# Delta rule: decay and key products of the chunk ahead placed inside the refinement steps, and its key blocks' transfers ahead of the inverse's

## The reference, cut to what matters

```python
def step(S, inputs):
    q_t, k_t, v_t, g_t, b_t = inputs
    S = S * jnp.exp(g_t)[..., None, None]
    kv = jnp.einsum('bhk,bhkv->bhv', k_t, S)
    u = b_t[..., None] * (v_t - kv)
    S = S + jnp.einsum('bhk,bhv->bhkv', k_t, u)
    o_t = jnp.einsum('bhk,bhkv->bhv', q_t * scale, S)
    return (S, o_t)
```

## Time and profile before

| what | us |
|---|---|
| median of 3 runs | 2779.55 |
| lowest, highest | 2772.53, 2780.12 |
| the profiled execution | 2775.25 |
| its span in the profile | 2773.5 |
| first to last `off_blocks` of the delta rule's loop | 226.85 to 514.07 |
| end of the delta rule's part, about | 559 |

### The profile page before, as it was taken

How to read it: one execution, slowest core, us unless ns; L and a number is a source line. 1 busy time by engine, 2 the same in 40 slices (tenths; PEclk the granted TensorE clock), 3 DMA queues, 4 the chain that set the end, 5 groups by cost and what they waited for, 6 DMA issues and landing times. The chain is left out here.

```text
span 2773.5 us, 34337 instructions
## 1 busy us (share of the span) xinstructions
PE 2623.4 (95%) x12650; PEld 1956.6 (71%) x12650; DVE 1653.6 (60%) x2474; ACT 883.1 (32%) x1342; POOL 380.4 (14%) x676
## 2 busy tenths in 40 slices
PE   8966988789999999999999989999999989999998
PEld 7845777778888888888888863333333678888886
DVE  6887787664444444544454377777776465655554
ACT  3343443231111111121112135666656322222221
POOL 0027787300000000000000022222210100000000
PEclk9988999899999999999999998999999999999999
DMA  2343232210000000000000024222220001000001
GB/s 92 102 137 76 56 80 53 50 46 23 24 23 23 23 23 23 23 23 23 23 23 23 1 54 73 71 73 70 73 81 32 31 16 47 30 31 15 15 16 46
DMA packets 104218, 122.32 MB, mean 44 GB/s; under 512 B 47454, under 2 KB 80478, under 8 KB 102438
## 3 DMA queue, kind: packets, MB, share of 16 engines
q1 hardware_dynamic: 104102, 120.79, 15.4%
HBM read 88.26 MB, written 24.64 MB: 41 GB/s over the span
## 5 line engine op out<-in xcount | busy, mean ns | idle before, releaser
L2282 DVE TENSOR_REDUCE att_top<-att_scores 128x1 f32<-128x1024 f32 x256 | 312.3, 1224 | 128.6 <-PE att_scores L2442 128.5
L296 DVE TENSOR_TENSOR fp_hidden<-fp_gelu,fp_up 128x512 f32<-128x512 f32 x128 | 88.1, 688 | 440.8 <-PE fp_up L75 377.8
L2155 ACT ACTIVATE att_probs<-att_scores 128x1024 f32<-128x1024 f32 x256 | 262.3, 1025 | 189.7 <-PE att_scores L2467 187.9
L2482 PE MATMUL att_out<-att_probs,att_padded 128*64 128x512 f32 x1024 | 269.0, 615 | 2.9 <-issue 2.8
L278 DVE TENSOR_TENSOR k_stream<-k_stream,fp_down 128x512 f32<-128x512 f32 x256 | 175.3, 685 | 84.0 <-PE fp_down L75 80.6
L356 ACT ACTIVATE fp_gelu<-fp_gate 128x512 f32<-128x512 f32 x128 | 76.3, 596 | 420.0 <-PE fp_gate L75 419.2
L73 PE MATMUL fp_gate<-fp_feat_hi,fp_w_hi 128*128 128x512 f32 x512 | 200.6, 392 | 3.8 <-DVE fp_feat_lo L266 3.8
L74 PE MATMUL fp_gate<-fp_feat_lo,fp_w_hi 128*128 128x512 f32 x512 | 200.1, 391 | 0.0
L75 PE MATMUL fp_gate<-fp_feat_hi,fp_w_lo 128*128 128x512 f32 x512 | 199.9, 391 | 0.0
L73 PE MATMUL fp_down<-fp_w_hi,fp_h_hi 128*128 128x512 f32 x512 | 199.3, 389 | 0.0
L75 PE MATMUL fp_up<-fp_feat_hi,fp_w_lo 128*128 128x512 f32 x512 | 199.2, 389 | 0.0
(11 more groups left out here) (339 smaller groups left out, 5570.9 us busy)
## 6 DMA issues: line engine op xcount, KB each, us to landing
f_early<-codes SPq DMA_DIRECT2D x16, 768.0 KB
f_early<-scales SPq DMA_DIRECT2D x16, 768.0 KB
att_stacks<-rotated SPq DMA_DIRECT2D x96, 128.0 KB
la_values<-w_sparse SPq DMA_DIRECT2D x10, 1024.0 KB, 4.8
f_early<-qkv SPq DMA_DIRECT2D x14, 576.0 KB, 6.0
att_stacks<-rotated SPq DMA_DIRECT2D x96, 64.0 KB
k_stream<-hidden SPq DMA_DIRECT2D x16, 256.0 KB, 4.5
att_stacks<-att_rot_hi SPq DMA_DIRECT2D x64, 64.0 KB
```

What stands on the lines that cost most here:

```text
L296: dve.tensor_tensor(hidden[:, c, :], gelu[:, c, :], up_ps[c][:], ALU.mult).then_inc(product_done, 1)
L2155: act.activation(probs[:, tile % PROBS, :], key_bank(tile)[:], ACT.Exp).then_inc(exp_done, 1)
L2282: dve.tensor_reduce(top[g % 2][:, STACK + t:STACK + t + 1], query_bank(tile)[:], AX.XY, ALU.max, negate=True).then_inc(max_done, 1)
L2482: last = pe.matmul(out[rows, :], padded[:, g % 2, t, :], probs[:, t, half * TB:(half + 1) * TB], start=t == 0, stop=t == T - 1)
```

## The change

On SP, `place_blocks` of the chunk ahead is issued before `take_inverse` of the next chunk, and not behind it. On PE, the decays of the chunk ahead stand between refinements 1 and 2, and its key products between refinement 2 and `apply_blocks`. ACT makes the exponents of the decays ahead of the copy of the solution, and the decay columns behind it. On DVE, `sum_keys` stands ahead of `low_output` and refinement 1, `norms` and `values_and_keys` ahead of refinement 2, and `key_blocks` right behind it, ahead of the additions to the stream. No instruction is added or taken away, and no wait's condition is changed.

```diff
@@ sync: blocks_of_chunks
                 if taken is not None:
                     take_blocks(taken)
+                    place_blocks(taken)
                 take_inverse(given, base_t, base_done, blocks_t, t_out, diag_in)
-                if taken is not None:
-                    place_blocks(taken)
                 place_inverse(given, blocks_t, t_out, diag, m_ps, diag_in)
@@ tensor: main loop
                 refine_solution(c, 1)
-                refine_solution(c, 2)
-                apply_blocks(c)
-                if c:
-                    project_output(c - 1, 0)
                 if ahead:
                     decays_between(ahead)
+                refine_solution(c, 2)
+                if ahead:
                     key_products(ahead)
+                apply_blocks(c)
+                if c:
+                    project_output(c - 1, 0)
                 turn_carried(c, ahead)
@@ scalar: main loop
                     norm_logs(ahead)
+                    exponent_of_decays(ahead)
                 copy_solution(c)
-                if ahead:
-                    exponent_of_decays(ahead)
-                    if ahead + 1 < CHUNKS:
-                        decay_columns(ahead + 1)
+                if ahead and ahead + 1 < CHUNKS:
+                    decay_columns(ahead + 1)
                 copy_carried(c)
@@ vector: main loop
                 refine_solution(c, 0)
+                if ahead:
+                    sum_keys(ahead)
                 if c:
                     low_output(c - 1)
                 refine_solution(c, 1)
                 if ahead:
-                    sum_keys(ahead)
+                    norms(ahead)
+                    values_and_keys(ahead)
                 refine_solution(c, 2)
                 if ahead:
-                    norms(ahead)
-                    values_and_keys(ahead)
+                    key_blocks(ahead)
                 if c == CHUNKS - 1:
                     first_codes(0, (0, 1, 2))
...
-                if ahead:
-                    key_blocks(ahead)
                 if c:
                     add_output(c - 1, 1)
```

More of the change, by code:

```diff
@@ L1313, in _ @@
                 refine_solution(c, 1)
+                if ahead:
+                    decays_between(ahead)
                 refine_solution(c, 2)
+                if ahead:
+                    key_products(ahead)
                 apply_blocks(c)
@@ L1317, in _ @@
                     project_output(c - 1, 0)
-                if ahead:
-                    decays_between(ahead)
-                    key_products(ahead)
                 turn_carried(c, ahead)
```

## The result

| | before | after |
|---|---|---|
| median, us | 2778.19 (4 runs) | 2814.74 (4 runs) |
| lowest, highest | 2772.53, 2780.12 | 2812.63, 2816.23 |
| ratio, 95% interval | | 1.0134, 1.0119 to 1.0149 |
| span of the profiled execution | 2773.5 | 2812.8 |

The change makes the kernel slower by 1.3%, 36.5 us in the medians and 39.3 in the spans. The forecast of 2801 had the direction and was 14 us short; the time lies 5.7 us above the range.

A forecast was written before the change was run, and what follows sets the result against it. The prediction took PE as nearly a bound, in a closed PE-DVE chain of 39.81 us a chunk, with POOL's last start setting the loop's end. 2775.25 + 16.2 (order) + 9.2 (clock) gave 2801 us, range 2785 to 2809.

The forecast's parts named there:

- The lost cover: Before PE's decays: DVE's norms, values and keys lose PE's cover; PE idles some 4.4 us, chain grows 4.71 a chunk.
- The first three signs: PE, six passes: 4.4 us wait before decays, released by DVE; first products 44.5 or 46 us apart, without inverse wait.
- Rivals 3 and 4: Loop: 3, even trade, stall under 1.7 us, within 8 us of 2775, chance 0.12; 4, POOL released, 2765, chance 0.08.
- The key blocks' moment: SP's transfer of key blocks: leaves 31.16 us after a chunk's first product, 30.53 before the change, so no earlier.
- SP's order: SP places blocks before taking the inverse: costs nothing in a long period, up to 3 us a chunk under 41.
- Rival 1: Loop: cover of norms, values and keys is lost and the clock falls with it; +25.4 us, 2801; chance 0.5.
- rival 2: Loop: same loss at full clock or with a fall in few passes; +16.2 us, 2791 (up to 2797); chance 0.3.
- the new chain: PE and DVE, from one refinement 0 to the next: 44.52 us a chunk at full clock, against a 41.58 period.
- sum of 25.4: Whole loop: +16.2 us at full clock plus 9.2 for the lower clock in six passes.
- the price of the clock: PE behind the new wait, each of six passes: 1.53 us more at the lower clock, +9.2 together.
- The bound of 2.55: PE, upper bound on the clock's cost per pass, from first products after 10.27 us of waiting: +15.3 together.
- ACT's term: ACT's decay columns ahead of the carried part's copy: up to 3.6 us in the first pass, zero from chunk 1.

The follow-up runs named there:

- e2: The kernel after with SP's old order, so only the orders on PE, ACT and DVE are changed; 2815.68 us, ratio 1.0142.
- e3: The kernel after with PE's decays moved behind refinement 2, DVE's and ACT's new order kept; 2785.87 us, ratio 1.0036.
- e1: The kernel before with SP's reorder alone, place_blocks ahead of take_inverse; 2778.73 us, ratio 1.0009.
- e8: The kernel before with SP's reorder from the second pass on, the first pass in the old order; 2777.63 us, ratio 1.0003.
- e7: The kernel after with four unread filling products on PE between refinement 1 and the decays; 2804.99 us, ratio 1.0102.
- e6: The kernel after with POOL's inverses of chunks 2 to 7 cut to one element per row and instruction, not computed; 2787.47 us, ratio 1.0048.
- e5: The kernel before with POOL's inverses of chunks 2 to 7 cut to one element per row and instruction, not computed; 2751.40 us, ratio 0.9912.
- the light pair: e5 and e6, the kernels before and after with POOL's inverses of chunks 2 to 7 cut; 2751.40 and 2787.47 us.
- e4: The kernel after with eight unread filling products on PE between refinement 1 and the decays; 2817.83 us, ratio 1.0152.

## Why the forecast had the direction and not the size

**The lost cover: right.** The first three signs that the prediction asked for are there: six waits ahead of the decays, released by DVE's keys, of 3.97 to 5.08 us (4.4 forecast); refinement 2 and all else of PE behind them; first products with no wait for the inverse. e2 puts the whole loss on the engines' order, and e3 takes 29 us of it away by moving the one step that the forecast named. Rivals 3 and 4 are out by this: no stall under 1.7 us, no release of POOL.

**The key blocks' moment: right in kind.** In chunk 3 of after SP's transfer leaves at 406.99, 34.8 us after the first product (31.16 forecast, 30.53 before). The blocks leave later than before the change, by all that the chain ahead of the key products grew. POOL's last start is 511.95 (486 or 495 forecast), and the last chunk's first products follow 44.6 us later (44.05 before).

**SP's order: right that it costs next to nothing**, by e1 and e8. The prediction costed it for a long period and left the first pass out. There it held one inverse back by 3.7 us in e1. In after this doesn't show, since the first pass is longer.

**Rival 1 or rival 2: the clock falls each time.** All six stretches of decays are long, 5.0 to 6.3 us from the decays' start to refinement 2, and never the 3.37 of the full clock. The Trainium skill (TensorE: Matmul & The Clock Gate, HAM oscillation) says that such a loop pays in every turn; this trace agrees, with six of six.

**What failed.** The chain and the wait were right, and the sizes of the terms were not. The prediction says of the change that "each costs what it did", and adds the new chain up from durations of the kernel before. In the new places DVE's instructions, and PE's behind the wait, took longer. Of the 16.2 us that its sum of 25.4 lacks, 9.4 are DVE's, 5.0 the clock's and 1.8 ACT's, as follows.

**The failed step, first: the price of the clock, 1.53 us.** It was taken from 24 products of 128 columns behind a 2.85 us wait, since the length of the wait was nearest. But the price does not follow from the length: in before the first products took 4.57 us behind 2.48 us of waiting, 4.28 behind 3.07, and 4.47 behind 22.75. Here, moreover, other shapes stand behind the wait. Six passes cost 5.58, 5.83, 5.02, 5.02, 6.28 and 5.60 us where 3.37 were forecast, 2.2 more on average: 13.1 us and not 9.2. The bound of 2.55 that the prediction had beside it would have been nearer for most of them. In e7 the six passes take 3.34 or 3.35 us each, and the 10 to 16 us that it gains enclose this sum.

**The failed step, second and larger: DVE's times from chunk 3 of before.** The prediction took each of DVE's steps from a single chunk. Four places of the chain from chunk 3 to chunk 4 of after, against it: from the last turned queries' end to DVE's start 422.55 - 420.30 = 2.25 where 1.68 were forecast; DVE's start to refinement 0, 381.78 - 374.48 = 7.30 for 6.72; refinement 0 to decays 392.12 - 381.78 = 10.34 for 9.64; decays to refinement 2, the clock, 5.02 for 3.37. The rest of the chunk, from refinement 2 to the last turned queries' end, is 23.16 for 23.11. The excess is 0.57 + 0.58 + 0.70 + 1.65 + 0.05 = 3.55, and 44.52 + 3.55 = 48.07 us, just the 422.55 - 374.48 between DVE's starts. No other wait has come into the chain here; only the sizes of its terms were off.

The longer ones are those that e6 shows short, so that POOL's work beside them is the cause. What differs between before and after is where they fall in POOL's inverse. In before the two multiplications of the state take 1.13 us in each of five chunks. They begin between 1.5 us ahead of the start of an inverse and 1.0 us behind it; at 386.23, for one, POOL pauses (382.91 to 387.71). At 346.42 POOL had already begun, and there the delay is on POOL's side. Its instruction of 48x60 elements took 0.69 us, where others of the same line and shape take 0.30:

```profile
346.42 1.13 DVE L1621 TENSOR_TENSOR dr_state<-dr_state,dr_e_all 64x384 f32<-64x384 f32 x2
```

```profile
346.44 0.69 POOL L1057 TENSOR_TENSOR f_blocks<-f_blocks,dr_base_tmp 48x60 f32<-48x60 f32 x1
```

In after they begin 5.0 to 7.4 us into an inverse, among instructions of POOL of 156 to 207 elements a row, and take 1.40 to 1.70 us. The sums of the keys take 2.37 to 2.44 us there, against 1.87 to 2.43 in before, where chunk 3 was among the shortest. Yet more chunks alone would not have mended the forecast: the means of the five chunks of before for DVE's start to refinement 0 (6.96, idle time left out), the sums (2.04) and the norms (3.14) give only 0.4 us a chunk more, and DVE's terms lacked 1.9.

Over all chunks that is what the sum lacks:

| term, us | forecast | measured | of it without the clock |
|---|---|---|---|
| first pass | 5.1 + 1.53 | 9.1 | 6.9 |
| four chunks | 4 x (2.94 + 1.53) | 4 x 7.35 = 29.4 | 4 x 5.18 = 20.7 |
| chunk 5's first product to POOL's last start | -0.7 + 1.53 | 3.1 | 0.9 |
| sum | 25.4 | 41.6 | 28.5 |

The first pass is 274.51 - 265.09 less the 0.33 by which the loop starts later. The sum is POOL's last start, 511.95 against 470.02, less the same. Of the 16.2 us that were missing, 3.9 are the clock's behind the decays' wait. Another 1.1 are the clock's as well: in chunks 1 and 4 DVE waited 0.57 us for the last products of refinement 1, which ran at the lower clock. In the first pass 1.8 are ACT's term, which the prediction put between 0 and 3.60 and took at 1.2. PE waits 2.99 us at 264.75 for the copy of the carried part, behind 3.61 us of decay columns. The remaining 9.4 are DVE's. From the sum to the 39.3 in the spans: 0.3 for the later start and 0.6 between POOL's last start and chunk 7's first product are added, and 3.2 come off behind it, 1.1 of them in chunk 7's first products (4.37 us for 5.49).

**What is shown and what is only argued.** That DVE's instructions take longer with POOL at work is shown by e5 and e6. That they escaped it in before by their place in POOL's inverse is read from five chunks of each kernel, and not tried by a run that shifts the inverse alone. How much of the 28.5 is the structure's and how much the longer instructions' is bounded by the light pair. There a chunk differs by 44.62 - 39.02 = 5.6 us. The clock's part is 2.1, since chunks 1 to 4 of e6 take 5.44 us on average from the decays to refinement 2, for 3.37. That leaves 3.5 for the lost cover (2.94 forecast), of the 5.18 that a chunk lost without the clock. About two thirds are thus the structure's and one third the longer instructions'.

**No version here beats the kernel before.** e3, the best form of the new order, is 0.36% slower. What bounds the kernel before is seen in e5: without POOL's work it would be 25 us faster, 13.7 of them behind chunk 6's first product, where it waits 10.27 us for the last inverse. And the key blocks' moment, which the change was to improve, hangs on DVE, whose refinements leave it no 3.1 us to spare.

## What to carry to other kernels

Before an engine's work is moved up to release a slower partner, find what covers it where it stands, and what is queued behind its wait where it will stand: here 3.1 us of DVE's work were hidden by two steps of PE, and moved ahead of them they stopped everything. A wait on PE costs its length and then the clock over what follows, so price that part with the shapes that stand behind the wait, not with those of the nearest wait. And a duration read from a trace holds for what the other engines did beside it. Before adding such durations up in a new order, look at what will run beside each of them there. A mean over more chunks of the old order does not show that: the multiplications of the state took 1.13 us in all five, and 1.40 to 1.70 in the new order.

## What the runs showed of the hardware

- DVE instructions take longer with POOL at work, small ones most of all. The same 128x24 scalar operation takes 581 ns on average in after, 280 in before and 190 with POOL light (e6). 128x384 products of two operands in SBUF take 950 ns in after, 844 in before and 554 in e6. The delay can also fall on POOL (0.69 us for 0.30, above). Reductions keep their 945 ns, and products with one operand in PSUM their 550 ns. The Trainium skill (SBUF — State Buffer, Who interferes with whom) says that a DVE instruction with two inputs in SBUF contends with a GpSimd instruction that reads SBUF, and that `tensor_reduce` on this chip never does; both agree with these rows. The 128x24 scalar operation has one input, and of such a one the same section of the Trainium skill says that it contends in its two-port mode only; no run here shows in which mode it was.
- The clock also fell behind waits of 2.0 us, which the forecast did not count. In after refinement 1 stands behind such a wait, the granted clock is 0.68 and 0.75 in the stretches 381:384 and 384:387, and its first 16 products take 3.01 us (1.95 for as many at 376.15 in the same chunk). In chunk 3 that cost nothing, since DVE comes last there; in chunks 1 and 4 DVE waited 0.57 us for it. In before the wait at that place was 1.16 us, and the 48 products of refinements 1 and 2 ran at 1.00 in 5.62 us. Behind the waits ahead of the decays, those of 3.20 us (e6) still went with decays of 5.00 to 6.12 us, and those of 1.1 to 1.7 us (e3) with 3.44.
- More work can take less time: four products that nobody reads, 3.6 us of PE's time a chunk, made a chunk 2.55 us shorter (e7), and eight made it no shorter (48.90 us, e4).
